# Spreading the attention's first preparation over the first FFN's last rounds, with an early flag for low parts and the weights' high parts first

## The chip, the cores and the metric

The kernel runs on one core of a Trainium2 chip. The metric is the device time of one execution in microseconds. The engines are TensorE (PE), VectorE (DVE), ScalarE (ACT), GpSimd (POOL) and SyncE (SP, which here only issues transfers). Each has a queue of its own that it works through in order; they meet through semaphores.

## The reference

A macaron block on x of 8 x 1024 rows of 128 numbers, in float32:

```
x = x + 0.5 * ffn(layernorm(x))
x = x + attn(layernorm(x))
x = x + 0.5 * ffn(layernorm(x))

ffn(x):  h = silu(x Wg^T / 127) * (x Wu^T / 127);  h Wd^T / 127     # hidden 384, int weights -127..127
attn(x): h = rmsnorm(x) * norm_w
         q, k, v = h Wq, h Wk, h Wv       # 4 query heads, 2 kv heads of 32
         q, k = l2norm(q), l2norm(k);  p = softmax(causal(q k^T * exp(log_temperature)))
         x + gate * (p v) Wo
```

## The kernel before

**Tiles.** x stays in SBUF as 64 tiles of 128 rows; a chunk `c` is four tiles, 512 rows, so there are NC = 16 chunks. Matrix products run in float16 with the inputs split into a high part and a low part (`hi`, the rounded value, and `lo`, the rest), which TensorE sums up. The integer weights are scaled by a power of two; their low part is zero unless an integer needs more bits than float16 has, and a flag, `loflag`, tells the engine's code whether to add its products. It is read into a register of TensorE, which then takes the `If` or the `Else` version of the whole FFN.

**FFN.** Each engine runs `pipeline`, a list of (offset, operation): in step i it does operation `op` for chunk i + offset. For a chunk: VectorE `stats` and `aggregate` (mean and variance), GpSimd `rstd`, ScalarE `normalise` (`XN`), TensorE `x_t` (transposes), ScalarE `x_hi`, VectorE `x_lo` (`XT`), TensorE `gate_` and `up`, ScalarE `silu` (`SG`), VectorE `hidden` (`H`), ScalarE `h_hi` (`HH`), GpSimd `h_lo` (`HL`), TensorE `down`, VectorE `residual`. TensorE's step is `gate_`(i+1), `down`(i-1), `up`(i+1), `x_t`(i+3). `H` and the other working tiles have two buffers. A step is called a round here, numbered by the chunk of its `H`. The argument `after` puts further work behind given steps.

**Attention.** A batch is two chunks ("halves"). Before its scores each half needs: statistics (`stats`, L787), reciprocal roots on GpSimd (`rstds`, L722), `normalise` (`AN`, L801, L806), `x_hi` (ACT, L646) and `x_lo` (POOL, L738) into `AS`, a transposing transfer by SP into `AXT`, the projection to q, k, v (`use`, L563, L580), `qkv_out` (ACT copies to `V` and squares to `SQ`, L652), `sums` and `norms` (DVE, L819, L827: three Newton steps for 1/norm), `unit` (`QN`, L844), `stack_hi` (ACT, L665), `stack_hi2` (DVE, L856), `stack_lo` (POOL, L743) into `ST`, and a second transposing transfer into `QKT`. `add_norm` (L810) adds the normalised input to x. The scores of a batch run in 12 groups `g`; the preparation of the next batch is laid between them, its projections in batch 0 at groups 3 and 4. For the first batch everything from the projection on happens after the FFN, in series. `by_heat` reads a second flag, `hotflag`, on each of four engines and takes the `If` or the `Else` version of the attention; with these inputs it is `Else`.

**Order in the queues.** VectorE does `stats` of the attention behind step 12 of the FFN, `normalise` and `attention_weights` behind step 15. TensorE waits for all residuals (`s_res`) before the attention. SP loads x first, then reads its flag when the attention weights are done, and then issues the transfers.

## Time and profile before

| what | value |
|---|---|
| time, median of 3 runs | 515.3 us (515.18 to 518.39) |
| profiled execution | 514.61 us, of it span 512.6 us |
| PE busy | 433.5 us (85%) |
| ACT busy | 387.7 us (76%) |
| DVE busy | 364.4 us (71%) |
| POOL busy | 244.1 us (48%) |
| chain that ended last | PE 62%, issue 11%, DVE 10%, POOL 6%, ACT 6%, DMA 3% |

Busy time is an average over the whole span; where a change acts, the windows and the timeline of that stretch count. "Issue" is time in which an engine waited for nothing that the profile shows.

### The profile page before, as it was taken

The page shows a single profiled execution, that of the slowest core. Times are in us where ns is not written, and L with a number is a line of the kernel's source. Part 1 is how long each engine was busy: PE and PEld are TensorE (multiplying, and loading weights), DVE is VectorE, ACT ScalarE, POOL GpSimd, SP SyncE. Part 2 cuts the span into 40 slices and gives each one's busy share as a digit, 9 for nine tenths or more (in the row PEclk, how much of TensorE's full clock was granted, in tenths as well). Part 3 has the DMA queues.
Part 4 walks back from the last instruction along what each step waited for, and adds up shares of the span by engine and source line. Part 5 has one row for each costly group of instructions (what it writes and reads, how often), then busy time and mean ns, then how long its engine had stood idle before and what let it go on. Part 6 is the DMA issues. An engine that isn't in the chain of part 4 may idle for free.

```text
span 512.6 us, 11225 instructions
## 1 busy us (share of the span) xinstructions
PE 433.5 (85%) x3862; PEld 234.4 (46%) x3862; DVE 364.4 (71%) x864; ACT 387.7 (76%) x552; POOL 244.1 (48%) x357
## 2 busy tenths in 40 slices
PE   0389999863088799999999999899999978999994
PEld 0237767552033253443443534434434334677674
DVE  4658887774761976886986968869755537888762
ACT  2388999631357789799788897987987977899971
POOL 4537777480264343526354454362030414777742
PEclk9999999995578999999999999999999998999998
DMA  6510000003242170711705207127060000212112
GB/s 183 168 42 3 0 0 0 1 1 47 45 81 41 32 134 2 133 35 37 130 0 108 56 0 140 25 44 122 1 120 6 2 3 1 60 44 61 52 52 61
DMA packets 85453, 26.54 MB, mean 52 GB/s; under 512 B 67872, under 2 KB 85408, under 8 KB 85408
## 3 DMA queue, kind: packets, MB, share of 16 engines
q1 hardware_dynamic: 84400, 25.76, 24.3%
q8 instruction: 26, 0.43, 0.4%
q10 hardware_dynamic: 1008, 0.20, 0.2%
q14 instruction: 19, 0.16, 0.1%
HBM read 4.98 MB, written 4.19 MB: 18 GB/s over the span
## 4 chain that ended last, share of the span: by engine, by line
PE 62%; issue 11%; DVE 10%; POOL 6%; ACT 6%; DMA 3%; POOLq 1%; SPq 0%; DVEq 0%; ACTq 0%
PE ps L384 14%; PE ps L553 11%; PE ps L534 9%; PE ps L558 9%; PE ps L424 5%; PE ps L418 5%; PE ps L377 2%; PE ps L446 2%; PE ps L580 2%; PE ps L538 2%; DVE X L815 2%; DMA AXT<-AS 1%; ACT PT L643 1%; POOL OL L227 1%; POOL HL L314 1%
## 5 line engine op out<-in xcount | busy, mean ns | idle before, releaser
L643 ACT ACTIVATE PT<-ps,k_exp 128x1024 f32<-128x1024 f32 (+1 forms) x192 | 162.7, 901 | 25.2 <-PE ps L538 19.9
L534 PE MATMUL ps<-QKT 128*128 128x512 f16 (+3 forms) x384 | 89.4, 335 | 25.0 <-DMA QKT<-ST 15.1
L384 PE MATMUL ps<-XT,WT 128*128 128x512 f16 x384 | 97.0, 391 | 8.4 <-issue 4.3
L314 POOL TENSOR_TENSOR HL<-H,HH 128x1024 f16<-128x1024 f32 x32 | 68.4, 2138 | 44.6 <-ACT HH L353 44.6
L553 PE MATMUL ps<-PT,V 128*32 128x512 f32 (+3 forms) x768 | 81.9, 498 | 0.4 <-ACT PVS L677 0.4
L558 PE MATMUL ps<-PT,ones 128*32 128x512 f32 (+3 forms) x768 | 79.6, 486 | 0.0
L263 DVE SCALAR_TENSOR_TENSOR H<-SG,k_isilu,ps 128x1536 f32<-128x1536 f32 x32 | 58.0, 1812 | 15.9 <-ACT SG L349 9.0
L534 PEld LDWEIGHTS ps<-QKT 128*128 128x128 f16 x384 | 28.4, 98 | 81.8 <-ACT PT L643 57.7
L227 POOL TENSOR_TENSOR OL<-ON,OH 128x512 f16<-128x512 f32 x16 | 19.5, 1218 | 95.9 <-ACT OH L223 95.9
L384 PEld LDWEIGHTS ps<-XT,WT 128*128 128x128 f16 x384 | 37.4, 100 | 45.4 <-issue 13.8
L217 DVE RECIPROCAL RD<-PVS 128x512 f32<-128x512 f32 x16 | 53.4, 3335 | 3.5 <-ACT PVS L677 3.5
L333 ACT ACTIVATE XN<-X,NB,RS 128x128 f32 (+1 forms) x128 | 52.4, 483 | 0.0
L349 ACT ACTIVATE SG<-ps,k_silu 128x1536 f32<-128x1536 f32 x32 | 48.8, 1526 | 3.5 <-PE ps L384 3.5
L746 POOL TENSOR_TENSOR ST<-QN,ST 128x512 f16<-128x512 f32 x16 | 20.0, 1252 | 59.6 <-ACT ST L669 59.6
L353 ACT ACTIVATE HH<-H 128x1024 f16<-128x1024 f32 x32 | 33.5, 1047 | 12.1 <-DVE H L263 12.1
L558 PEld LDWEIGHTS ps<-PT,ones 128*32 128x32 f32 x768 | 24.8, 110 | 37.5 <-issue 32.1
L268 DVE SCALAR_TENSOR_TENSOR X<-ps,k_ffn,X 128x512 f32<-128x512 f32 (+1 forms) x32 | 24.0, 750 | 23.8 <-PE ps L424 23.8
L424 PE MATMUL ps<-WD,H 128*128 128x128 f32 x256 | 37.3, 291 | 0.0
L538 PE MATMUL ps<-causal,ident 128*128 128x128 bf16 x256 | 34.9, 222 | 0.0
L821 DVE TENSOR_REDUCE SS<-SQ 128x24 f32<-128x768 f32 x16 | 15.1, 943 | 27.7 <-ACT SQ L662 27.7
L306 POOL TENSOR_TENSOR RS<-RS,nhalf 128x4 f32<-128x4 f32 x32 | 33.4, 1044 | 2.5
L580 PE MATMUL ps<-QKVO,AXT 128*128 128x256 f16 x192 | 25.5, 288 | 9.9 <-DMA AXT<-AS 9.9
(117 smaller groups left out, 696.0 us busy)
## 6 DMA issues: line engine op xcount, KB each, us to landing
X<-in_L_attn_x SPq DMA_DIRECT2D x16, 256.0 KB, 3.0
result<-X SPq DMA_DIRECT2D x16, 256.0 KB, 2.3
AXT<-AS SPq DMA_TRANSPOSE x16, 3.1
QKT<-ST SPq DMA_TRANSPOSE x16, 5.6
w_int<-in_L_ffn_w_gate SPq DMA_DIRECT2D x1, 192.0 KB, 3.7
w_int<-in_L_ffn_w_up SPq DMA_DIRECT2D x1, 192.0 KB, 4.1
w_int<-in_L_ffn_w_down SPq DMA_DIRECT2D x1, 192.0 KB, 4.6
qkvo<-in_L_attn_Wq ACTq DMA_DIRECT2D x1, 64.0 KB, 3.3
```

The source lines that it names most:

```text
L217: e.reciprocal(RD[:, :], PVS[:, 1, :]).then_inc(a_rd, 1)
L263: e.scalar_tensor_tensor(H[k % 2][:, :, :], SG[:, :, :], k_isilu[:, 0:1], U, ALU.mult, ALU.mult).then_inc(s_h, 1)
L314: e.tensor_tensor(HL[k % 2][:, :, :], H[k % 2][:, NW:, :], HH[k % 2][:, :, :], ALU.subtract).then_inc(s_hl, 1)
L333: i = e.activation(XN[k % 2][:, t, :], tile(c, t), ACT.Identity, bias=NB[k % 2][:, t:t + 1], scale=RS[k % 2][:, t:t + 1])
L349: e.activation(SG[:, :, :], G, ACT.Silu, scale=k_silu[:, 0:1]).then_inc(s_silu, 1)
L384: i = e.matmul(out[:, j, :], WT[:, wp, w * NJ + j, :], XT[k % 2][:, xp, :], start=a == 0, stop=a == len(passes) - 1)
L424: i = e.matmul(DN[:, t, :], H[k % 2][:, j, t * P:(t + 1) * P], WD[:, j, :], start=False, stop=j == NW - 1, skip_group_check=True)
L534: i_ = e.matmul(o, QKT[k % 2][:, i // TPC, NH + hp, i % TPC * P:(i % TPC + 1) * P], QKT[k % 2][:, qc, 2 * hp + h, CH - n:CH], start=True, ...
L538: i_ = e.matmul(SCORES[hp][:, h, 0:P], ident16[:, :], causal[:, :], start=False, stop=True, skip_group_check=True)
L553: e.matmul(PVD[HD * h:HD * h + HD, 0, CH - n:CH], V[k % 2][:, i, v0:v0 + HD], PT[g % 2][:, h, 0:n], start=i == 0, stop=done, skip_group_ch ...
L558: i_ = e.matmul(PVD[HD * h:HD * h + HD, 1, CH - n:CH], ones32[:, :], PT[g % 2][:, h, 0:n], start=i == 0, stop=done, skip_group_check=True)
L643: e.activation(PT[g % 2][:, 2 * hp:2 * hp + 2, 0:n], SCORES[hp][:, :, 0:n], ACT.Exp, scale=k_exp[:, 0:1]).then_inc(a_exp, 1)
```

## The change

- **Early flag.** Instead of looking at the low parts of the weights, VectorE compares the largest absolute integer with 2048, right after the column maxima. The maximum comes over TensorE in a second small transpose.
- **High part of the weights first.** VectorE makes the high part straight from the float weights, TensorE transposes it (parts 0 and 1, copied by ScalarE), and the low part follows (parts 2 and 3, copied by VectorE). `x_t`, `x_hi` and `x_lo` of chunk 0 come ahead of that. ScalarE runs one small silu early. Both flags are read into registers early.
- **Attention weights** are made ahead of step 0 of the FFN, not behind step 15.
- **Preparation of the first batch spread out.** VectorE: `stats` behind steps 7 and 8, `normalise` in four pairs of tiles behind steps 10 to 13. GpSimd: `rstds` in two parts each behind steps 8 to 11, `x_lo` behind 13 and 14. ScalarE: `x_hi` behind 12 and 14. The statistics have a buffer of their own, `abns`.
- **Joined.** SP issues both `AXT` transfers before its branch. The first projections stand in TensorE's queue behind `up` 15 and behind `down` 14 and write into PSUM banks that the FFN has left. ScalarE's `qkv_out` of half 0 comes between the last silu and the last `h_hi`. VectorE's `units` (sums, norms of one half at a time, `QN`, copies) stand behind step 15, the last `residual` and `add_norm` follow, and then the branch. TensorE waits for the last `residual` only behind the first scores.

TensorE at the start, before: the names are `ident` for the unit matrix, `w_nat` for the weights, `XN0` and `XN1` for the buffers of the normalised x.

```order
L1161 MATMUL ps<-ident32,m4 128x4
L1168 MATMUL ps<-ident16,w_nat 128x128 x18
L1171 MATMUL ps<-ident32,lomax 1x128
L377 MATMUL ps<-ident32,XN0 128x128 x4
L1176 TENSOR_LOAD loflag
L1176 ISA x2
L1179 COMPARE_AND_BRANCH
L377 MATMUL ps<-ident32,XN1 128x128 x4
```

TensorE at the start, now:

```order
L1248 MATMUL ps<-ident32,m4 128x4
L396 MATMUL ps<-ident32,XN0 128x128 x4
L1008 TENSOR_LOAD hotflag
L1008 ISA x2
L1253 TENSOR_LOAD loflag
L1253 ISA x2
L1261 MATMUL ps<-ident16,w_nat 128x128 x18
L1265 COMPARE_AND_BRANCH
L396 MATMUL ps<-ident32,XN1 128x128 x4
```

The x transpose of chunk 0 and both flag loads moved ahead of the weights' transposes; the branch stayed between them and chunk 1.

VectorE in rounds 10 to 13, now (`X` is written by `residual`):

```order
L276 SCALAR_TENSOR_TENSOR H0<-SG,k_isilu,ps 128x1536
L267 TENSOR_TENSOR XT0<-ps,XT0 128x512
L250 BN_STATS bns<-X 128x6 x4
L281 SCALAR_TENSOR_TENSOR X<-ps,k_ffn,X 128x512
L262 BN_AGGR MV1<-bns 128x2 x4
L858 TENSOR_SCALAR AN0<-X,AMV0,RMS0 128x128 x2
L276 SCALAR_TENSOR_TENSOR H1<-SG,k_isilu,ps 128x1536
L267 TENSOR_TENSOR XT1<-ps,XT1 128x512
L281 SCALAR_TENSOR_TENSOR X<-ps,k_ffn,X 128x512
L858 TENSOR_SCALAR AN0<-X,AMV0,RMS0 128x128 x2
```

The pairs of `AN` stand between a `residual` and the next `H`. Before, all eight stood behind the last `H`:

```order
L263 SCALAR_TENSOR_TENSOR H1<-SG,k_isilu,ps 128x1536
L268 SCALAR_TENSOR_TENSOR X<-ps,k_ffn,X 128x512
L806 TENSOR_SCALAR AN0<-X,AMV0,RMS0 128x128 x4
L806 TENSOR_SCALAR AN1<-X,AMV1,RMS1 128x128 x4
L1131 TENSOR_SCALAR qkvo<-qkvo,ipw 128x256
```

TensorE at the join, now, in the `Else` version (`AXT0` is half 0):

```order
L403 MATMUL ps<-XT1,WT 128x512 x6
L612 MATMUL ps<-QKVO,AXT0 128x256 x12
L445 MATMUL ps<-WT,HH0 128x128 x8
L445 MATMUL ps<-WT,HL0 128x128 x8
L451 MATMUL ps<-WD,H0 128x128 x4
L612 MATMUL ps<-QKVO,AXT1 128x256 x12
L445 MATMUL ps<-WT,HH1 128x128 x8
L445 MATMUL ps<-WT,HL1 128x128 x8
L451 MATMUL ps<-WD,H1 128x128 x4
```

The projections, which stood behind the last `down` and the branch, now stand ahead of `down` 14 and `down` 15. The diff, cut to its core:

```diff
-        w_bank = [bank[2][:, 0, :], bank[2][:, 1, :], bank[0][:, 1, :]]
+        w_bank = [bank[2][:, 0, :], bank[2][:, 1, :], bank[3][:, 1, :], bank[1][:, 1, :]]
+        w_parts = [(0, 2 * NJ), (2 * NJ, 3 * NJ), (3 * NJ, 3 * NJ + 8), (3 * NJ + 8, 6 * NJ)]
...
+            def first_out(k, c):
+
+                if ph == 0 and k == NC - 1:
+                    project_out()
...
+                if ph == 0 and k == 0:
+                    e.wait_ge(s_wt, 1)
+                    if low:
+                        e.wait_ge(s_wtl, 2)
...
+        FIRST_BANKS = [XP] + [ps[:, i, :] for i in range(3)]
...
+            if first_half is not None:
+
+                e.wait_ge(s_silu, NC)
+                for c in range(2):
+                    use(None, None, ("qkv", first_half, c))
+                return
+            first = [u for k, u in seq if k is None and u[0] != "qkv" and u[:2] != ("m", 1)]
+            late = [u for k, u in seq if k is None and u[0] != "qkv" and u not in first]
+
+            e.wait_ge(a_cp, 4)
+            e.wait_ge(s_h, NC)
+            if shift:
+                e.wait_ge(s_res, NC)
+                for u in first:
+                    use(None, None, u)
             scores(0, 0, 0, 0)
             scores(0, 0, 0, 1)
+            e.wait_ge(s_res, NC)
...
+            if first == "units":
+
+                sums(0, 0)
+                norms(0, 2, 0, 1)
+                unit(0, 10, 0, 0)
+                sums(1, 1)
+                stack_hi2(0, 0)
+                norms(10, 4, 1, 2)
+                unit(0, 20, 1, 1)
+                stack_hi2(1, 1)
+                return
...
+            hot = is_hot(e)
+            for half in range(2):
+                turn_x(e, half)
+            by_heat(e, turn, hot)
...
                             ALU.add).then_inc(s_wd, 1)
-            ffn_pool(e, 0, None, {NC - 3: lambda: att_pool(e, ("rstds", 0)),
-                               NC - 2: lambda: att_pool(e, ("rstds", 1)),
-                               NC - 1: lambda: [att_pool(e, ("x_lo", h)) for h in range(2)]})
+            ffn_pool(e, 0, None, {NC - 8: lambda: att_pool(e, ("rstds_a", 0)),
+                                  NC - 7: lambda: att_pool(e, ("rstds_b", 0)),
+                                  NC - 6: lambda: att_pool(e, ("rstds_a", 1)),
+                                  NC - 5: lambda: att_pool(e, ("rstds_b", 1)),
+                                  NC - 3: lambda: att_pool(e, ("x_lo", 0)),
+                                  NC - 2: lambda: att_pool(e, ("x_lo", 1))}, 4)
...
+            hot = is_hot(e)
+            ffn_act(e, 0, 1)
+            for r in range(2):
                 e.wait_ge(s_wpe, 3 + r)
-                lo, hi = 8 * r, min(8 * r + 8, 6 * NJ)
-                src = w_bank[r].bitcast(f16).rearrange("p (j n) -> p j n", n=P)
-                e.activation(w16[:, lo:hi, :], src[:, 0:hi - lo, :], ACT.Copy).then_inc(s_wt, 1)
+                lo, hi = w_parts[r]
+                e.activation(w16[:, lo:hi, :], w_part(r), ACT.Copy).then_inc(s_wt, 1)
             e.wait_ge(s_wready, 1)
-            ffn_act(e, 0, None, {NC - 1: lambda: [att_act(e, False, ("x_hi", h)) for h in range(2)]})
+            ffn_act(e, 0, None, {NC - 4: lambda: att_act(e, False, ("x_hi", 0)),
+                                 NC - 2: lambda: att_act(e, False, ("x_hi", 1)),
+                                 NC - 1: lambda: att_act(e, False, ("qkv_out", 1))},
+                    1, lambda: att_act(e, False, ("qkv_out", 0)))
+            for half in range(2):
+                att_act(e, False, ("stack_hi", half))
             e.wait_ge(s_wready, 2)
-            by_heat(e, att_act)
+            by_heat(e, att_act, hot)
             ffn_act(e, 1)
 
...
+            e.tensor_tensor(colmax[:, 4:5], colmax[:, 0:1], colmax[:, 1:2], ALU.max)
...
+            link(e.tensor_reduce(lo1[:, :], bank[0][0:1, 1, 0:P], AXX, ALU.max))
+            e.tensor_scalar(loflag[:, :], lo1[:, :], 2048.0, None, ALU.is_gt).then_inc(s_low, 1)
...
-            link(e.tensor_scalar(w_flt[:, 0:2 * NJ, :], w_flt[:, 0:2 * NJ, :], ipw[:, 0:1], None,
-                                 ALU.mult))
-            link(e.tensor_scalar(w_flt[:, 2 * NJ:, :], w_flt[:, 2 * NJ:, :], ipw[:, 1:2], None,
-                                 ALU.mult))
-            link(e.tensor_copy(w_nat[:, 0, :, :], w_flt[:, :, :]))
-            e.tensor_tensor(w_nat[:, 1, :, :], w_flt[:, :, :], w_nat[:, 0, :, :], ALU.subtract)\
-                .then_inc(s_wprep, 1)
+            cuts = [(0, 2 * NJ), (2 * NJ, 3 * NJ)]
+            for c, (lo, hi) in enumerate(cuts):
+                i = e.tensor_scalar(w_nat[:, 0, lo:hi, :], w_flt[:, lo:hi, :], ipw[:, c:c + 1], None, ALU.mult)
+            i.then_inc(s_wprep, 1)
+            ffn_dve(e, 0, 2)
             e.wait_ge(s_wprep, 3)
-            e.tensor_reduce(lomax[:, :], w_nat[:, 1, :, :].rearrange("p a b -> p (a b)"), AXX,
-                            ALU.max, apply_absolute_value=True).then_inc(s_wprep, 1)
-
+            for c, (lo, hi) in enumerate(cuts):
+                i = e.scalar_tensor_tensor(w_nat[:, 1, lo:hi, :], w_flt[:, lo:hi, :], ipw[:, c:c + 1],
+                                           w_nat[:, 0, lo:hi, :], ALU.mult, ALU.subtract)
+            i.then_inc(s_wprep, 1)
             link(e.tensor_scalar(k_silu[:, :], pw[:, 0:1], 1.0 / 127.0, None, ALU.mult))
             link(e.reciprocal(k_isilu[:, :], k_silu[:, :]))
             link(e.tensor_scalar(k_ffn[:, :], k_silu[:, :], k_silu[:, 0:1], 0.5 / 127.0, ALU.mult,
                                  ALU.mult))
-            link(e.tensor_scalar(k_ffn[:, :], k_ffn[:, :], pw[:, 1:2], None, ALU.mult))
-            e.wait_ge(s_wpe, 6)
-            link(e.tensor_reduce(lo1[:, :], bank[1][0:1, 1, 0:P], AXX, ALU.max))
-            e.tensor_scalar(loflag[:, :], lo1[:, :], 0.0, None, ALU.is_gt).then_inc(s_wready, 1)
+            e.tensor_scalar(k_ffn[:, :], k_ffn[:, :], pw[:, 1:2], None, ALU.mult).then_inc(s_wready, 1)
+            for r in range(2, 4):
+                e.wait_ge(s_wpe, 3 + r)
+                lo, hi = w_parts[r]
+                e.tensor_copy(w16[:, lo:hi, :], w_part(r)).then_inc(s_wtl, 1)
+            e.wait_ge(s_wready, 1)
...
+            flags = []
+            def weights_and_flag():
+                attention_weights()
+                flags.append(is_hot(e))
+            ffn_dve(e, 0, None, {-1: weights_and_flag,
+                                 NC - 9: first_rows("stats", 0),
+                                 NC - 8: first_rows("stats", 1),
+                                 NC - 6: first_rows("normalise", 0, (0, 2)),
+                                 NC - 5: first_rows("normalise", 0, (2, TPC)),
+                                 NC - 4: first_rows("normalise", 1, (0, 2)),
+                                 NC - 3: first_rows("normalise", 1, (2, TPC)),
+                                 NC - 1: lambda: att_dve(e, False, "units")}, 4)
+            for half in range(2):
+                first_rows("add_norm", half)()
+            by_heat(e, att_dve, flags[0])
             ffn_dve(e, 1)
         @block.tensor
         def _(e):
             e.wait_ge(s_const, 2)
             e.wait_ge(s_wprep, 1)
-            e.matmul(bank[0][0:4, 0, 0:P], colmax[:, :], ident32[:, :], is_transpose=True,
+            e.matmul(bank[0][0:4, 0, 0:P], colmax[:, 0:4], ident32[:, :], is_transpose=True,
+                     start=True, stop=True)
+            e.matmul(bank[0][0:1, 1, 0:P], colmax[:, 4:5], ident32[:, :], is_transpose=True,
                      start=True, stop=True).then_inc(s_wpe, 1)
             e.wait_ge(s_wprep, 2)
             e.matmul(bank[1][:, 0, 0:4], m4[:, 3:4].to_broadcast([4, P]), ident32[0:4, 0:4],
                      start=True, stop=True).then_inc(s_wpe, 1)
-            e.wait_ge(s_wprep, 3)
+            ffn_pe(e, 0, 0, 0)
+            hot = is_hot(e)
+            e.wait_ge(s_low, 1)
+            low = e.value_load(loflag[0:1, 0:1], min_val=0, max_val=1)
             blocks = [(s, j) for s in range(2) for j in range(3 * NJ)]
-            for r in range(3):
+            for r in range(4):
+                if r in (0, 2):
+                    e.wait_ge(s_wprep, 3 + r // 2)
                 dst = w_bank[r].bitcast(f16)
-                for a, (s, j) in enumerate(blocks[8 * r:8 * r + 8]):
+                for a, (s, j) in enumerate(blocks[slice(*w_parts[r])]):
                     i = e.transpose(dst[:, a * P:(a + 1) * P], w_nat[:, s, j, :], ident16[:, :])
                 i.then_inc(s_wpe, 1)
-            e.wait_ge(s_wprep, 4)
-            e.matmul(bank[1][0:1, 1, 0:P], lomax[:, :], ident32[:, :], is_transpose=True,
-                     start=True, stop=True).then_inc(s_wpe, 1)
-            ffn_pe(e, 0, 0, 0)
-            e.wait_ge(s_wt, 3)
-            e.wait_ge(s_wready, 1)
-            low = e.value_load(loflag[0:1, 0:1], min_val=0, max_val=1)
-
-            def ffn(ph):
+            def ffn(ph, after={}):
                 with e.If(low > 0):
-                    ffn_pe(e, ph, 1)
+                    ffn_pe(e, ph, 1, None, after)
                 with e.Else():
-                    ffn_pe(e, ph, 0)
-            ffn(0)
-
-            e.wait_ge(s_res, NC)
-            e.wait_ge(s_wready, 2)
-            by_heat(e, att_pe)
+                    ffn_pe(e, ph, 0, None, after)
+            def first_projection(half):
+                e.wait_ge(s_wready, 2)
+                att_pe(e, False, half)
+            ffn(0, {NC - 2: lambda: first_projection(0), NC - 1: lambda: first_projection(1)})
+            by_heat(e, att_pe, hot)
             ffn(1)
```

## Rows read from the trace of the kernel before

**Rows 1.** Windows of core 0: from:to in us, length, busy us of each engine (x instructions), PEclk, DMA share, GB/s.

```profile
60.00:100.00 40.00, 39.77 (x324) 27.79 (x321) 33.43 (x87) 34.43 (x53) 26.03 (x33) 1.00 0.00 0
130.00:140.00 10.00, 0.00 (x0) 0.00 (x0) 7.77 (x18) 2.91 (x3) 3.06 (x3) 0.50 0.19 36
219.98:253.90 33.92, 32.26 (x322) 14.41 (x320) 27.29 (x61) 29.35 (x41) 15.94 (x22) 1.00 0.37 63
```

**Rows 2.** Timeline of the start: start us, us, engine, line, operation [idle before <-releaser].

```profile
16.20 2.10 PE L1168 MATMUL ps<-ident,w_nat 128*128 128x128 f16 x18 [4.19 <-DVE w_nat L1114]
17.27 2.21 ACT L1067 ACTIVATE WT<-ps 128x1024 f16<-128x1024 f16 x3 [7.35 <-PE ps L1168]
...
24.59 1.09 PE L377 MATMUL ps<-ident,XN 128*128 128x128 f32 x4 [5.23 <-issue]
...
31.59 1.81 DVE L263 SCALAR_TENSOR_TENSOR H<-SG,k_isilu,ps 128x1536 f32<-128x1536 f32 x1 [3.37 <-PE ps L384]
```

**Rows 3.** Timeline, TensorE's jump into the second FFN.

```profile
422.71 4.44 PE L384 MATMUL ps<-XT,WT 128*128 128x512 f16 x12 [3.40 <-issue]
```

**Rows 4.** Timeline of one round in the middle of the first FFN.

```profile
85.14 1.81 DVE L263 SCALAR_TENSOR_TENSOR H<-SG,k_isilu,ps 128x1536 f32<-128x1536 f32 x1 [0.18 <-ACT SG L349]
...
88.61 0.75 DVE L268 SCALAR_TENSOR_TENSOR X<-ps,k_ffn,X 128x512 f32<-128x512 f32 x1 [1.05 <-PE ps L424]
88.62 2.14 POOL L314 TENSOR_TENSOR HL<-H,HH 128x1024 f16<-128x1024 f32 x1 [1.05 <-ACT HH L353]
...
90.01 1.81 DVE L263 SCALAR_TENSOR_TENSOR H<-SG,k_isilu,ps 128x1536 f32<-128x1536 f32 x1 [0.65 <-ACT SG L349]
```

**Rows 5.** Timeline of the first FFN's last rounds.

```profile
94.14 0.86 DVE L793 BATCH_NORM_STATS2 bns<-X 128x6 f32<-128x128 f32 x4
...
96.66 1.78 DVE L263 SCALAR_TENSOR_TENSOR H<-SG,k_isilu,ps 128x1536 f32<-128x1536 f32 x1
...
99.61 2.13 POOL L314 TENSOR_TENSOR HL<-H,HH 128x1024 f16<-128x1024 f32 x1 [3.98 <-ACT HH L353]
...
105.79 1.81 DVE L263 SCALAR_TENSOR_TENSOR H<-SG,k_isilu,ps 128x1536 f32<-128x1536 f32 x1 [0.60 <-PE ps L384]
```

**Rows 6.** One line, L806, from 108 to 116 us: duration ns min/median/max.

```profile
L806 DVE TENSOR_SCALAR AN<-X,AMV,RMS x8: 333/336/2142, 109.7 to 113.3; 128x128 f32<-128x128 f32 x8
```

**Rows 7.** Chain of waits through the join: start us, us, what.

```profile
106.95 1.07 PE ps L418 x16
108.02 0.96 PE ps L424 x8
...
109.75 4.84 DVE AN L806 x8
...
117.95 0.17 DVE k_exp L1142
...
119.48 3.87 DMA AXT<-AS
...
129.60 0.96 DVE SS L821
...
133.26 0.97 DVE QN L850
...
137.09 5.65 DMA QKT<-ST
```

**Rows 8.** Timeline of the attention's first groups.

```profile
140.10 0.86 DVE L793 BATCH_NORM_STATS2 bns<-X 128x6 f32<-128x128 f32 x4
...
142.78 1.04 PE L534 MATMUL ps<-QKT 128*128 128x512 f16 x2 [15.06 <-DMA QKT<-ST]
...
144.29 1.12 DVE L806 TENSOR_SCALAR AN<-X,AMV,RMS 128x128 f32<-128x128 f32 x4 [1.53 <-POOL RMS L734]
...
150.75 1.14 ACT L650 ACTIVATE AS<-AN 128x512 f16<-128x512 f32 x2
...
156.41 1.90 PE L580 MATMUL ps<-QKVO,AXT 128*128 128x256 f16 x12 [2.00 <-DMA AXT<-AS]
```

209 lines of the change are left out of this document (107 added, 102 removed).

## The prediction

> **What bounds the kernel now.** I read the windows first, then the timeline of the weak stretches, then the chain of waits through them. In the first FFN's middle TensorE is busy for 39.77 of 40 us, so nothing is to be had there except by doing less; between 130 and 140 us it does nothing at all, and the granted clock there is 0.50, its 1.2 GHz level [rows 1]. Two places hold the idle time. At the start, TensorE ends the transposes of the weights at 18.3, ScalarE's last copy of them ends at 19.48, and the second x transpose starts only at 24.59, with 5.23 us of idle time that no semaphore explains ("issue") [rows 2]. At the join of the first FFN and the attention, the last `H` starts at 105.79 [rows 5] and the first scores start at 142.78, after 15.06 us of waiting for the `QKT` transfer [rows 8]: 37.0 us. The chain there runs in series through `AN`, the attention weights, the `AXT` transfer, the projection, sums, norms, `QN` and the `QKT` transfer [rows 7]. Each is short; they are long only because nothing lies beside them.
>
> All sums below are made against the profiled execution: 512.6 us of span, 514.61 in all, 0.7 below the median of 515.3. Stated times of the changed kernel are on the old time axis until the sum; a gain at the start shifts them all.
>
> **1. The start: about 1.8 us less.** The gap of 19.48 to 24.59 holds the flag's load and the jump into the FFN's code. SP does its own flag load, its branch and a DMA issue from 118.12 to 119.48, so load and branch together are at most 1.4 us and the load alone about 0.8; that leaves 4.3 us for TensorE's jump [rows 2, 7]. A second jump of TensorE into such a branch left it idle for 3.40 us [rows 3]. The change loads both flags before the weights' transposes, where TensorE waited 4.19 us for VectorE anyway [rows 2], so the load costs nothing as long as that wait is there; without it, it would cost 0.8 for each flag. The jump stays, after the 18 transposes. Their low half comes later than before, since VectorE now makes it after the high half and `x_lo`; I put their end at 18.1 against 18.3, so the second x transpose starts at 18.1 + 4.3 = 22.4, 2.2 earlier. ScalarE's `XN` must be there too, after its weight copies; it is at about 19.5 and does not bind. Against this, VectorE now makes the attention weights before the first `H`: 118.12 - 114.59 = 3.5 us [rows 7], plus a flag load of 0.8, into a wait of 3.37 [rows 2]. `H` starts 0.9 late, and half of that reaches ScalarE's next silu. Net 2.2 - 0.4 = 1.8. The bounds are 0 (the fetch ends when it ended before) and 4.6 (the jump is hidden: 24.59 - 19.5, less 0.5).
>
> The Trainium skill (Advanced Engine Details and Errata, Control Flow Timing) puts a compare-and-branch at about 108 ns. No row here shows TensorE doing it so fast; by that figure the start would gain 4.6 instead of 1.8.
>
> **2. The rounds: about 4.6 us more.** A round of the FFN takes 90.01 - 85.14 = 4.87 us from `H` to `H` [rows 4]. From round 12 on that pace would put the last `H` at 90.01 + 3 x 4.87 = 104.6; it is at 105.8, so the two blocks of statistics of before, beginning at 94.14 and holding the next `H` back to 96.66, cost 1.2 net [rows 5]. The change puts much more into the rounds.
> - Statistics behind rounds 7 and 8: 2 x 1.3 us on VectorE (94.14 to the second block at 95.46, half of the stretch to 96.66) [rows 5]. VectorE waits 0.65 before an `H` [rows 4], and ScalarE takes the `H` 0.5 later than it could; the rest, 1.5, stretches the loop.
> - Pieces of `rstds` on GpSimd: some 1.7 and 1.35 us each, twice, against 1.05 us of idle time before each `HL` [rows 4]. `HL` gets late by 0.3 to 0.7 a round.
> - The normalisation in four pairs, each behind a `residual`. One such operation takes 0.34 us, or 2.14 when it is caught beside GpSimd's `HL` [rows 6], which itself takes 2.14 [rows 4]. `residual` starts at 88.61 and `HL` at 88.62 in the same round [rows 4], so VectorE comes to the pair just when `HL` has begun. The round then is `H` 1.8, to `HL` 1.15 (99.61 - 98.44) [rows 5], `HL` 2.1, and the pair 0.67: 5.7 us. Three rounds at 5.7 cost 2.5 over the pace, and the first, in which the `rstds` pieces add up, 1.7.
>
> Together 1.5 + 1.7 + 2.5 = 5.7 over the pace, less the 1.2 that before paid: the last `H` starts 4.6 later, at 110.4. The bounds are 0 and 7.
>
> **3. From the last `H` to the first scores: 37.0 becomes 17.8, so 19.2 us less.** `AXT` of half 0 has landed (half 0 is ready a round earlier; issue plus landing is 3.87 [rows 7]), so TensorE does the first projection, 1.9 us for its 12 products [rows 8], then `down` of round 14, 1.07 + 0.96 [rows 7], and VectorE the `residual`, 0.75 [rows 4], since it lies ahead of `units` in VectorE's queue: 4.7. Sum and norms as before, 133.26 - 129.60 = 3.7; half the width saves little where ten short operations follow each other. From `QN` to the `QKT` issue 137.09 - 133.26 = 3.8, and the transfer 5.65 to the scores [rows 7, 8]. 4.7 + 3.7 + 3.8 + 5.65 = 17.8. Half 1 lies beside this, as do `down` 15 and GpSimd's last `HL`. The second projection stands ahead of `down` 15 in TensorE's queue and waits for `AXT` half 1; that delays `add_norm` and no scores. The bounds are 16 (the sums do not wait for the residual) and 22 (half 1's chain or GpSimd's `HL` gets in between).
>
> **4. Behind the join: about 4.7 us given back.** Before, the statistics for the next batch began at 140.10, 2.7 us ahead of the scores, and the first half of `AN` was complete at 144.29 + 1.12 = 145.4; ScalarE took it at 150.75 [rows 8]. Now VectorE first does half 1's norms and `QN`, its copies, the last `residual` and eight operations of `add_norm` (2.3 at 0.28 each [rows 8]): by the durations of part 3 that ends 3.6 us after the first scores. Then it jumps into the attention's code. Before, that jump lay in VectorE's idle time. Priced as TensorE's 3.40 [rows 3], the statistics begin 7.0 after the scores instead of 2.7 before; `AN`'s first half, 5.3 later (145.4 - 140.1), passes ScalarE, GpSimd and SP (the 5.66 of 150.75 to 156.41 [rows 8]) and meets TensorE's projection for the next batch at 18.3 instead of 13.6. TensorE waited 2.00 there already [rows 8], so it all counts: 4.7. With a jump of 0.5 it would be 1.8; those are the bounds, with 0.5 more above for ScalarE's own jump and table load ahead of the first exponential.
>
> **Sum:** -1.8 + 4.6 - 19.2 + 4.7 = -11.7. 514.6 becomes 502.9, and 515.3 becomes **503.6 us**. The shorter gap may also save up to 1 us of products at the 1.2 GHz level; I leave it to the range.
>
> **The rivals.**
> - *The jumps are cheap.* For it: no loop of VectorE or ScalarE shows an "issue" wait of that kind. Against it: [rows 2, 3]. Start -4.6, give-back 1.8: 515.3 - 4.6 + 4.6 - 19.2 + 1.8 = 497.9. Chance 0.18.
> - *The pairs get in ahead of `HL`.* `residual` and `HL` start 0.01 us apart [rows 4]; if GpSimd is pushed later by its own new pieces, VectorE's pairs run at 0.67 and `HL` waits for no more than one of them. The rounds then cost 1.5, not 4.6: 500.5. The Trainium skill (SBUF — State Buffer, Who interferes with whom) has it that the one that issues first keeps the shared port and the other blocks; the row with 2.14 agrees for the case in which GpSimd was first, and none shows the other. Chance 0.10.
> - *The join is longer.* GpSimd's last `HL`, the late second projection or `stack_lo` get in between: 22 instead of 17.8, 507.8. Chance 0.15.
> - *The early flag brings nothing,* since the jump ends when it did: 505.4. Chance 0.05.
> - *Slower than before.* VectorE enters the attention 7 us late and stays late: the projections for the six batches after the next wait for their `AXT` too. At 4.7 each the total is 503.6 + 6 x 4.7 = 531.8; it decides from (520.5 - 503.6) / 6 = 2.8 us a batch. Against it: VectorE is busy for 27.29 of 33.92 us in a batch [rows 1], so 6.6 idle us catch up 4.7 in one batch. Chance 0.04.
>
> My forecast has 0.45; 0.03 is left for the gain being used up by something that I do not see, at 510 to 520. About 1% (5 us) is what a measurement of this kernel tells from no change. Faster by more: 0.45 + 0.18 + 0.10 + 0.15 + 0.05, less 0.02 for their upper tails, is 0.91; within 1% 0.05; slower 0.04. The range of 496 to 510 reaches from a little below the cheap jumps (both faster rivals at once would give 494.8) to the longer join with 2 us on top.
>
> **What would show it.** The second x transpose of the start at 22.4 (19.5 if jumps are cheap, 24.6 if nothing moved). `AN` operations of 2 us next to `HL`, and rounds of 5.7 us from round 10 on. 17.8 us from the last `H` to the first scores, with the sums released by the `residual`. VectorE idle with "issue" behind `add_norm`, and a wait of some 6.7 us of TensorE before the first projection of the attention's loop. Batches of 33.9 us after that. The forecast is wrong if the rounds stretch by much more than 1.5 us each, since four engines have almost no slack in them, or if the waits at batch boundaries grow.

## The result

| kernel | median of the runs | profiled execution | its span | granted clock |
|---|---|---|---|---|
| before | 515.24 us (514.79 to 518.39) | 514.61 us | 512.6 us | |
| changed | 497.03 us (495.16 to 498.07) | 498.07 us | 496.3 us | 0.972 |

The ratio is 0.9637, interval [0.9592, 0.9681]: 18.2 us less, where 11.7 was forecast. The direction and the range were right, and so was the sign of each of the four terms; the likeliest value was 6.6 us too high, and all four terms of the sum erred to the same side. The profiled execution is the slowest of the changed kernel's runs and that of before is a little below its median, so the two profiles differ by 16.3 us of span, and the terms are measured in these spans.

### The profile page after: what moved, and what is told of

Same layout as the page of the kernel before. It is cut to its first block, busy times and chain, and to the rows that moved or that the text cites. A ratio compares the mean times of both kernels' runs of the same rounds, so it can differ in the third digit from the quotient of the medians.

```text
span 496.3 us, 11174 instructions
## 1 busy us (share of the span) xinstructions
PE 433.1 (87%) x3862; PEld 232.3 (47%) x3862; DVE 369.8 (75%) x876; ACT 386.9 (78%) x552; POOL 244.0 (49%) x357
## 4 chain that ended last, share of the span: by engine, by line
PE 59%; DVE 14%; issue 11%; POOL 7%; ACT 5%; DMA 2%; POOLq 1%; DVEq 1%; SPq 0%; ACTq 0%
PE ps L403 13%; PE ps L585 11%; PE ps L590 9%; PE ps L566 9%; PE ps L451 5%; PE ps L445 5%; PE ps L474 2%; DVE X L868 2%; PE ps L396 2%; DVE H L276 2%; PE ps L570 2%; ACT SG L362 2%; PE ps L612 1%; POOL OL L240 1%; POOL RMS L786 1%
## 5 line engine op out<-in xcount | busy, mean ns | idle before, releaser
L585 PE MATMUL ps<-PT,V 128*32 128x512 f32 (+3 forms) x768 | 83.6, 507 | 1.3 <-ACT PVS L721 1.3
L858 DVE TENSOR_SCALAR AN<-X,AMV,RMS 128x128 f32<-128x128 f32 (+1 forms) x64 | 33.8, 593 | 3.5 <-POOL RMS L786 3.5
L451 PEld LDWEIGHTS ps<-WD,H 128*128 128x128 f32 x256 | 32.0, 196 | 0.0
```

Source lines behind the costliest of these rows:

```text
L451: i = e.matmul(DN[:, t, :], H[k % 2][:, j, t * P:(t + 1) * P], WD[:, j, :], start=False, stop=j == NW - 1, skip_group_check=True)
L585: e.matmul(PVD[HD * h:HD * h + HD, 0, CH - n:CH], V[k % 2][:, i, v0:v0 + HD], PT[g % 2][:, h, 0:n], start=i == 0, stop=done, skip_group_ch ...
```

## The profile after

Landmarks of each trace carry the whole comparison. H0, H1, H15: starts of the first `H`s and the last one of the first FFN; S: first scores; P: first projection for the third pair of halves ("batch 2"); F: first product of the second FFN. The columns behind H15 are stretches, in us.

| profile | second x transpose | H1 | H15 | H15 to S | S to P | P to F | F to end | span |
|---|---|---|---|---|---|---|---|---|
| before | 24.59 | 36.49 | 105.79 | 36.99 | 45.30 | 234.63 | 89.89 | 512.6 |
| changed | 21.52 | 32.87 | 105.44 | 17.12 | 48.61 | 234.39 | 90.74 | 496.3 |
| start alone | 21.36 | 34.50 | 103.79 | 37.48 | 44.72 | 234.65 | 90.56 | 511.2 |
| flag late | 24.11 | 35.46 | 107.91 | 17.09 | 47.68 | 234.09 | 89.73 | 496.5 |
| pairs ahead of `HL` | 20.19 | 31.54 | 100.86 | 17.11 | 48.20 | 234.23 | 89.80 | 490.2 |
| low swapped | 19.66 | 31.17 | 103.64 | 19.01 | 46.98 | 231.07 | 92.90 | 493.6 |
| hot swapped | 21.57 | 32.93 | 105.41 | 17.08 | 47.54 | 239.71 | 90.76 | 500.5 |
| exp early | 21.07 | 32.42 | 104.99 | 17.13 | 50.62 | 234.65 | 89.91 | 497.3 |
| stats early | 21.44 | 32.77 | 105.25 | 17.09 | 48.30 | 234.55 | 89.81 | 495.0 |
| these five together | 19.72 | 31.25 | 100.58 | 17.07 | 47.71 | 234.33 | 90.71 | 490.4 |
| changed, again | 21.36 | 32.70 | 105.17 | 17.10 | 49.36 | 234.11 | 87.86 | 493.6 |
| adds early | 20.94 | 32.28 | 104.86 | 17.09 | 49.62 | 234.07 | 90.76 | 496.4 |
| exp and adds early | 21.08 | 32.42 | 104.89 | 17.11 | 49.16 | 234.10 | 90.84 | 496.1 |
| best | 19.22 | 30.73 | 100.06 | 19.27 | 46.56 | 231.06 | 92.05 | 489.0 |

The changed kernel stands there twice: between its two profiles S to P differs by 0.75 and F to end by 2.9. Smaller differences in those columns tell nothing. The four terms, changed against before: start -3.6 (H1), rounds +3.3 (H1 to H15), join -19.9, behind the join +3.9 (S to the end). The last one is the least certain: against the second profile of the changed kernel it would be +1.5, and up to P alone it is +3.3 in the one and +4.1 in the other.

**The start**, timeline: start, duration, engine, line, operation, idle time before and what ended it.

```profile
16.91 1.14 PE L1261 MATMUL ps<-ident,w_nat 128*128 128x128 f16 x9 [0.91 <-DVE w_nat L1189]
...
21.52 1.09 PE L396 MATMUL ps<-ident,XN 128*128 128x128 f32 x4 [3.47 <-issue]
...
28.50 1.81 DVE L276 SCALAR_TENSOR_TENSOR H<-SG,k_isilu,ps 128x1536 f32<-128x1536 f32 x1 [0.86 <-issue]
```

The transposes end at 18.05 (forecast 18.1), then come 3.47 us of idle time without the flag's load; [rows 2] had 5.23 with it. The jump itself is not the same in every program with this start: 3.40 in e9, 2.75 in e10 and 2.42 in e3.

**The rounds**, the four pairs of `AN` on VectorE and `HL` on GpSimd.

```profile
81.17 2.13 POOL L327 TENSOR_TENSOR HL<-H,HH 128x1024 f16<-128x1024 f32 x1
81.91 1.73 DVE L858 TENSOR_SCALAR AN<-X,AMV,RMS 128x128 f32<-128x128 f32 x2
...
86.54 2.52 DVE L858 TENSOR_SCALAR AN<-X,AMV,RMS 128x128 f32<-128x128 f32 x2
86.59 2.13 POOL L327 TENSOR_TENSOR HL<-H,HH 128x1024 f16<-128x1024 f32 x1
...
91.95 2.13 POOL L327 TENSOR_TENSOR HL<-H,HH 128x1024 f16<-128x1024 f32 x1 [1.95 <-ACT HH L366]
92.02 2.40 DVE L858 TENSOR_SCALAR AN<-X,AMV,RMS 128x128 f32<-128x128 f32 x2
...
97.97 2.67 DVE L858 TENSOR_SCALAR AN<-X,AMV,RMS 128x128 f32<-128x128 f32 x2
```

Each pair meets `HL` and takes 1.73 to 2.67 us instead of 2 x 0.34 [rows 6]; the fourth meets `x_lo` of GpSimd as well (from 99.41, 1.16 us). This is what the forecast said from one row with 2.14. The rounds from H10 on take 6.15, 5.42, 5.37, 6.22 and 4.87 us; the three from H7 to H10, which hold the statistics, take 15.35 together, where before took 14.52.

**The middle of the FFN and the join**, windows (from:to, length, busy us of PE, PEld, DVE, ACT, POOL, PEclk, DMA share, GB/s).

```profile
60.00:100.00 40.00, 37.82 (x298) 25.66 (x297) 37.84 (x86) 32.76 (x48) 30.63 (x43) 1.00 0.00 1
110.00:120.00 10.00, 3.46 (x36) 2.88 (x36) 9.20 (x28) 2.88 (x4) 3.51 (x3) 0.86 0.13 30
```

Against [rows 1], VectorE went from 33.43 to 37.84 busy us of 40, TensorE from 39.77 to 37.82: the two are as busy as each other over this window, part of VectorE's time being the wait beside `HL`. From the first pair (81.91) to H14 (100.57) VectorE waits once, 0.56 us, so there it has become the bound. At the join VectorE is now busy for 9.20 of 10 us, so that stretch is VectorE's too. Its chain of waits (start, us, what):

```profile
105.50 1.47 PE ps L612 x12
...
108.85 0.75 DVE X L281
109.60 0.87 DVE SS L874
...
113.86 0.96 DVE QN L900
```

`H` to sums 4.2 (forecast 4.7), sums to `QN` 4.3 (3.7; one operation of it, L877 on 24 columns, took 1.17 us, and 0.24 for the other half: it ran beside GpSimd's last `HL`, from 109.51 to 111.64, and ended with it), from there to the issue of the `QKT` transfer at 117.83 4.0 (3.8), and 4.7 to the scores at 122.56 (5.65): 17.1 against 17.8. As forecast, the residual of round 14 stands ahead of the sums.

**Behind the join**, timeline of ScalarE, VectorE and TensorE.

```profile
123.84 1.28 ACT L687 ACT_TABLE_LOAD   x1 [2.20 <-issue]
125.13 2.12 ACT L687 ACTIVATE PT<-ps,k_exp 128x1024 f32<-128x1024 f32 x2
...
135.53 0.63 ACT L694 ACTIVATE AS<-AN 128x512 f16<-128x512 f32 x1 [1.87 <-DVE AN L858]
```

```profile
122.98 0.74 DVE L281 SCALAR_TENSOR_TENSOR X<-ps,k_ffn,X 128x512 f32<-128x512 f32 x1
123.64 2.12 DVE L868 TENSOR_SCALAR X<-X,A,B 128x128 f32<-128x128 f32 x8
126.12 0.87 DVE L845 BATCH_NORM_STATS2 abns<-X 128x6 f32<-128x128 f32 x4 [0.35 <-issue]
...
133.43 2.06 DVE L858 TENSOR_SCALAR AN<-X,AMV,RMS 128x128 f32<-128x128 f32 x4 [1.99 <-POOL RMS L786]
```

```profile
126.39 0.80 PE L566 MATMUL ps<-QKT 128*128 128x384 f16 x2 [1.53 <-ACT PT L687]
128.27 1.94 PE L585 MATMUL ps<-PT,V 128*32 128x512 f32 x8
129.98 1.42 PE L590 MATMUL ps<-PT,ones 128*32 128x512 f32 x8
...
138.41 1.47 PE L612 MATMUL ps<-QKVO,AXT 128*128 128x256 f16 x12 [0.22 <-DMA AXT<-AS]
```

Three engines are late here at once. ScalarE jumps and loads its table, so the first exponential comes 2.57 us after the scores (before: 1.29). VectorE's statistics come 3.56 after them (before: 2.68 ahead). And TensorE's products with `V` and with the ones take 1.94 and 1.42 us for eight where the same ones took 1.06 and 1.04 before, since they now fall into the stretch with a granted clock of 0.50, its 1.2 GHz level (0.50 from 127.5 to 130.5, 0.87 in the next microsecond). Windows from the scores on, of the changed kernel:

```profile
122.56:127.56 5.00, 3.46 (x13) 1.47 (x14) 4.51 (x20) 3.52 (x4) 1.12 (x3) 0.50 0.70 152
127.56:132.56 5.00, 5.00 (x36) 1.78 (x38) 2.32 (x13) 2.36 (x4) 4.53 (x12) 0.68 0.05 12
```

and of the kernel before:

```profile
142.78:147.78 5.00, 4.82 (x24) 2.10 (x28) 1.50 (x6) 3.56 (x4) 4.60 (x11) 0.57 0.68 128
147.78:152.78 5.00, 5.00 (x64) 2.03 (x53) 4.83 (x24) 3.46 (x7) 1.32 (x2) 1.00 0.01 2
```

TensorE was busy for 4.82 of the first five us before and is for 3.46 now, with the pause of 1.53 ahead of the x384 scores in it; the full level of the clock comes later. The projection for batch 1 comes at 15.85 after the scores (16.57 in the second profile of the changed kernel); 13.63 before, 18.3 in the forecast.

What releases its `AXT` transfer (issued at 134.93) is GpSimd's `x_lo`, 133.74 to 134.90. Two chains reach that operation within 0.05 us of each other (0.3 in e9): ScalarE's `AS`, which stands behind a late exponential and ends at 133.66, and GpSimd's own queue, in which both halves' `rstds` stand ahead of it, from 127.48 to 133.71. Taking one of the two away leaves the other.

## The experiments

Each was timed beside the kernel before on the same chip (medians there 515.96 for e1 to e4, 517.26 for e5 to e8, 514.55 for e9 to e11, 514.66 for e12). The chips differ by more than some effects, so what is compared with the changed kernel is the ratio to before, 0.9637 [0.9592, 0.9681] there, and the stretches of the profiles. Of the variants of the changed kernel only e8 and e11 are clear of it by the ratio alone.

**e1_start_only.** The kernel before with the start of the changed one and nothing else: high part first, early flag, chunk 0 ahead of the weights, attention weights still behind step 15.

```diff
+        w_parts = [(0, 2 * NJ), (2 * NJ, 3 * NJ), (3 * NJ, 3 * NJ + 8), (3 * NJ + 8, 6 * NJ)]
+            e.tensor_scalar(loflag[:, :], lo1[:, :], 2048.0, None, ALU.is_gt).then_inc(s_low, 1)
+            ffn_pe(e, 0, 0, 0)
+            e.wait_ge(s_low, 1)
+            low = e.value_load(loflag[0:1, 0:1], min_val=0, max_val=1)
```

> The kernel before with the new start alone (early low-part flag, high parts of the weights first, chunk 0 transposed early); the attention's preparation stays behind the FFN. Theory A: the start and the rest of the change add up. In the changed kernel the FFN's second H is 3.6 us earlier than before (32.87 against 36.49), and here the attention weights do not stand before the first H, so I expect a gain of 3.5 to 4.5 us, about 511 us. Theory B: the start's gain is used up by a wait later in the FFN and only counts together with the joined preparation: under 1 us of gain.

513.11 us (511.23 to 513.87), ratio 0.9944 [0.9917, 0.9972]: 2.9 us less, and in the profile 2.0 by H1 and by H15. That is less than the changed kernel's 3.6 by H1, and the difference has a place:

```profile
21.36 1.09 PE L386 MATMUL ps<-ident,XN 128*128 128x128 f32 x4 [3.30 <-issue]
22.23 1.06 PE L393 MATMUL ps<-XT,WT 128*128 128x512 f16 x2
24.79 4.45 PE L393 MATMUL ps<-XT,WT 128*128 128x512 f16 x10 [1.50 <-issue]
```

A second pause of 1.50 us lies behind the first two gate products; the changed kernel has none. Why, no run here tells. All of the start's gain arrives at H15, so the rounds hand it on in full.

**e2_flag_late.** The changed kernel with the low flag loaded where it was.

```diff
-            e.wait_ge(s_low, 1)
-            low = e.value_load(loflag[0:1, 0:1], min_val=0, max_val=1)
...
+            e.wait_ge(s_wt, 2)
+            e.wait_ge(s_wtl, 2)
+            e.wait_ge(s_wready, 1)
+            low = e.value_load(loflag[0:1, 0:1], min_val=0, max_val=1)
```

> The changed kernel, but TensorE reads the low-part flag behind the weights' transposes and copies, where the kernel before read it. Theory A: the flag's position is worth its load (about 0.8 us) and the wait for the copies (0.9 us), since the jump stays where it is: second x transpose at 23.0 to 23.5 instead of 21.5, total 1.5 to 2 us longer. Theory B: the load's latency is the whole gap of the kernel before, and the jump costs nothing: second x transpose at 24.5, 3 us longer.

499.02 us (497.84 to 499.73), 0.969 [0.9628, 0.9752]. The second x transpose starts at 24.11, near the 24.5 of theory B, behind 6.13 us of "issue". That does not make the jump free: 3.47 of it stand there without the load too. The load, with the waits that the edit puts ahead of it, accounts for the other 2.7, where theory A had 1.7. The early load is worth 2.6 us there, in H1, and 2.5 in H15; in the medians 2.0.

**e3_pairs_first.** The pairs of `AN` stand behind `x_lo` and ahead of the `residual` in the same rounds, so that `HL` has not begun.

```diff
+            def pair(k, c):
+                if ph == 0 and 10 <= k <= 13:
+                    h, part = divmod(k - 10, 2)
+                    att_dve(e, False, ("normalise", h, (2 * part, 2 * part + 2)))
...
-            pipeline(e, [(0, hidden), (2, x_lo), (1, last_o_norm), (5, stats), (5, sums_there),
+            pipeline(e, [(0, hidden), (2, x_lo), (0, pair), (1, last_o_norm), (5, stats), (5, sums_there),
```

> The changed kernel with each pair of AN operations one place earlier in VectorE's queue: behind x_lo and ahead of the residual, in the same rounds 10 to 13. Same work. Theory A (the pair is caught beside GpSimd's HL, 1.7 to 2.7 us instead of 0.67): the pairs take 0.6 to 0.7 us each, rounds 11 to 14 shrink from 5.4-6.2 to about 4.9-5.1, and the last H is 3 to 4 us earlier; total about 493.5. Theory B (the rounds are long because of the added work, wherever it stands): the last H moves by less than 1 us.

493.68 us (492.01 to 494.49), 0.959 [0.9531, 0.9649].

```profile
78.41 0.59 DVE L863 TENSOR_SCALAR AN<-X,AMV,RMS 128x128 f32<-128x128 f32 x2
79.82 0.75 DVE L281 SCALAR_TENSOR_TENSOR X<-ps,k_ffn,X 128x512 f32<-128x512 f32 x1
79.85 2.13 POOL L332 TENSOR_TENSOR HL<-H,HH 128x1024 f16<-128x1024 f32 x1
...
88.46 0.61 DVE L863 TENSOR_SCALAR AN<-X,AMV,RMS 128x128 f32<-128x128 f32 x2 [0.25 <-POOL RMS L791]
```

The same instructions take 0.59 to 0.61 us a pair instead of 1.73 to 2.67, and H1 to H15 takes 69.32, as in the kernel before (69.30), where it took 72.57. H10 to H15 is where it is gained: 24.78 instead of 28.03. So the whole +3.3 of the rounds is taken back by moving the pairs away from `HL`. Statistics and `rstds` are not free for that: H7 to H10 takes 15.35, 0.8 more than before, as in the changed kernel, and H10 to H15 still some 0.5 more than before without its own statistics (25.51 less their 1.2). They cost together what before paid for its statistics. By the medians e3 is 3.4 below the changed kernel, by the ratios 2.4, and its profile also has a start that is 1.3 earlier, which the edit does not touch.

**e4_low_swapped.** TensorE's two versions of the FFN change places, so that the one in use is the `If`.

```diff
-                with e.If(low > 0):
-                    ffn_pe(e, ph, 1, None, after)
+                with e.If(low < 1):
+                    ffn_pe(e, ph, 0, None, after)
```

> The changed kernel with the two versions of the FFN swapped in TensorE's code: the version that runs (no low part) comes straight behind the branch, the other behind it. Theory A: the 3.47 us before the second x transpose and the 1.73 us before the second FFN's first product are TensorE's jump to code that is far away; straight on, the transpose comes at 19.3 (released by XN) and the second FFN starts 1.5 us earlier. Total 3 to 4 us less. Theory B: the wait is that of a branch itself or of the new code in any case, near or far: no change.

495.42 us (493.64 to 495.52), 0.9608 [0.9547, 0.9669].

```profile
19.66 1.11 PE L396 MATMUL ps<-ident,XN 128*128 128x128 f32 x4 [1.30 <-ACT XN L346]
```

No "issue" is left ahead of the second x transpose: a semaphore of ScalarE releases it now. The pause ahead of the second FFN is gone as well (P to F 231.07 instead of 234.39). So the pause belongs to the jump over the unused version. The trace's DMA records say what lies in it: in the changed kernel's pauses a packet of 16 KB of the queue named "instruction" is fetched (18.84 to 19.96 at the start, 402.91 to 404.01 ahead of the second FFN), and in e4 none is in either place. The other programs agree: one in each such pause, none where the near version follows (the starts of e8 and e11).

The total fell by 1.6 us by the medians and 1.5 by the ratios, not by the 3 to 4 expected. Ahead of the second FFN little of the gain is kept: the first `H` there now stands directly behind VectorE's other work.

```profile
407.08 0.38 DVE L262 BATCH_NORM_AGGREGATE MV<-bns 128x2 f32<-128x6 f32 x4
407.38 1.78 DVE L276 SCALAR_TENSOR_TENSOR H<-SG,k_isilu,ps 128x1536 f32<-128x1536 f32 x1
```

P to this `H` is 237.75, against 239.73 and 238.44 in the two profiles of the changed kernel. And something took part of the start's gain back: the `QKT` transfers, issued at the same distance from H15, landed after 6.1 to 6.5 us instead of 4.6 to 5.5, and the scores came 1.9 later. Two "instruction" packets run at once over the issue of the first of these transfers in e4 and e11 (the later one ends 1.1 us behind it); in the changed kernel and in e8 the last one has ended before. That they are the cause was not tested.

**e5_hot_swapped.** The same for the attention's two versions, on all four engines that have them.

```diff
-            with e.If(hot > 0):
-                att(e, True)
+            with e.If(hot < 1):
+                att(e, False)
```

> The changed kernel with the two versions of the attention swapped in the code of TensorE, VectorE, ScalarE and SP: the one that runs comes straight behind the branch. Theory A: the 2.20 us (issue) of ScalarE between stack_hi and the table load ahead of the first exponential is its far jump, and now lies on the path; it vanishes, the first exponential starts 1.3 us earlier (1.2 instead of 2.6 after the first scores begin), and total time falls by 1 to 2 us. Theory B: ScalarE waits there for something else, or the later AXT wait makes up for it: under 0.5 us.

502.17 us (499.93 to 503.12), 0.9712 [0.9648, 0.9776]: 5.1 us more than the changed kernel by the medians, 3.9 by the ratios. The first exponential came at 1.27 as hoped, but the jump only moved to where the attention is left:

```profile
409.74 5.28 PE L403 MATMUL ps<-XT,WT 128*128 128x512 f16 x12 [8.46 <-issue]
415.11 1.81 DVE L276 SCALAR_TENSOR_TENSOR H<-SG,k_isilu,ps 128x1536 f32<-128x1536 f32 x1 [5.44 <-issue]
```

TensorE stands still for 8.46 us there, instead of 3.16 in the changed kernel. It makes two far jumps in a row, out of the attention and into the `Else` version of the second FFN, and three "instruction" packets of 16 KB begin in the pause (401.64, 405.23, 405.60). The exit alone is no dearer than the other jumps, as e8 shows, where the FFN's near version follows:

```profile
399.69 4.37 PE L408 MATMUL ps<-XT,WT 128*128 128x512 f16 x12 [3.09 <-issue]
```

Two jumps cost 8.46, more than 3.09 and 3.16 together; why was not tested. VectorE's 5.44 is no jump: its `H` needs the products that TensorE begins at 409.74 and ends at 415.02. The pause lies between two stretches that have TensorE full.

**e6_exp_early.** ScalarE does one exponential of a single column between its two `stack_hi`, so that the table is loaded before the jump.

```diff
+            e.activation(warm[:, :], lt_t[:, :], ACT.Exp)
```

> The changed kernel with one tiny exponential on ScalarE between the two stack_hi, where it is idle, so that the table load of 1.28 us happens there and not ahead of the first scores' exponential. If that load is on the path behind the join, the first exponential starts 1.2 us earlier relative to the scores and the total falls by about 1.2 us; if the batch's AXT sets the time instead (the projection for batch 1 came 15.85 us after the scores, 2.2 later than before), it changes nothing.

496.14 us (492.93 to 499.07), 0.9584 [0.9519, 0.965]. The exponential came at 1.27, yet P came at 50.62: no gain in this profile, which is the slowest of the four runs; the ratio leaves room for a small one. `AS` of the first half is made 1.5 us earlier against the scores, but GpSimd's `x_lo` for it is not:

```profile
131.14 0.63 ACT L694 ACTIVATE AS<-AN 128x512 f16<-128x512 f32 x1
...
133.18 0.20 POOL L788 TENSOR_TENSOR B<-rv,AMV 128x4 f32<-128x4 f32 x1
133.33 1.15 POOL L792 TENSOR_TENSOR AS<-AN,AS 128x512 f16<-128x512 f32 x1
```

It stands behind the `rstds` of both halves in GpSimd's queue, and the `AXT` transfer goes out at 134.50, 12.38 after the scores. So here the late statistics carry the term, through GpSimd.

**e7_stats_early.** Statistics for batch 1 directly behind `units`, ahead of the jump.

```diff
                 stack_hi2(1, 1)
+                stats(2, 2, 0)
+                stats(3, 3, 1)
                 return
```

> The changed kernel with the statistics for batch 1 ahead of the last residual and add_norm in VectorE's queue, directly behind units. My prediction put the give-back behind the join at 4.7 us, through the late statistics. If that path (statistics, reciprocal roots, AN, AS, AXT, projection) carries the 3.3 us that are lost by batch 1, then bringing the statistics forward by 3 us brings the projection to 13.6 instead of 15.85 us after the scores and the total down by 2 us. If the late exponentials and the low granted clock carry it, the total falls by under 0.5 us.

496.29 us (491.98 to 497.7), 0.9586 [0.951, 0.9662]. The statistics came 3.1 us earlier, the `AXT` transfer for batch 1 at the same 12.39 after the scores: the second `AN` started at 133.31, as in the changed kernel (133.43), again behind GpSimd. GpSimd's `rstds` start as late as before, now released by `add_norm`, which still reads `A` and `B` that `rstds` writes:

```profile
127.27 0.28 POOL L777 TENSOR_TENSOR rv<-AMV,eps_ln 128x4 f32<-128x4 f32 x1 [3.85 <-DVE X L868]
```

The edit has a side effect too: the last `residual` comes behind the statistics, and TensorE waits 1.53 us for it behind the first scores.

**e8_all.** e3 to e7 in one kernel.

> The changed kernel with all of it: pairs ahead of the residual, both versions swapped, the early exponential, the early statistics. If the pieces lie one after the other on the path: 3.3 (pairs) + 2.7 (swapped FFN) + 2 to 3 (behind the join) = 8 to 9 us below the changed kernel, about 488.5. If the ones behind the join overlap: about 490.5.

492.43 us (491.33 to 493.15), 0.9532 [0.9473, 0.9591]. That is 1.9 above the more cautious of the two expectations. It has e3's rounds; the swapped attention takes back what the swapped FFN gives (P to F 234.33).

**e9_after_again.** The changed kernel beside the next two.

> The changed kernel itself, on the chip of the next two, as their yardstick. Both theories: 496 to 498 us, first attention scores some 122.5 us into the span, the transfer that transposes for batch 1 issued 12.4 us after them, the projection of batch 2 at +48.6.

496.15 us (495.44 to 496.97), 0.966 [0.9591, 0.9729].

**e10_add_early.** e7, and `add_norm` of both halves behind the last two `H`, ahead of the residual and of the jump.

```diff
+            def add_first(k, c):
+                if ph == 0 and k >= NC - 2:
+                    h = k - (NC - 2)
+                    att_dve(e, False, ("add_norm", h))
```

> VectorE does both additions of the norm (add_norm) of the first two batches in its queue behind the last two H, ahead of its far jump, and statistics for the third and fourth batch directly behind the last round. Theory A (what is given back behind the join comes by the chain add_norm, then GpSimd's rstds, then ScalarE's AN, then the transfer that transposes): that transfer for batch 1 is issued at about +10 us behind the first scores instead of +12.4, the first projections at about +13.6, batch 2's at +46 to +47, and the kernel takes about 2 us less than the changed kernel, near 495. Rival B (TensorE's granted clock in that stretch, or the order on ScalarE, sets it): the statistics come early, the projections stay where they are, and the time is within 0.5 us of the changed kernel. Rival C: the additions wait for their inputs and hold up the residual of the last rounds, and the first scores come more than 1 us later.

497.67 us (496.64 to 498.44), 0.9679 [0.9607, 0.975], 1.5 us above e9 on the same chip and inside the noise: no gain. GpSimd is free early here (its last `rstds` operation ends at 130.0), and `AN` did come early, complete at 131.2, so the wait of `rstds` for `add_norm` is real. It alone does not set the transfer, since `AS` was not made:

```profile
125.00 0.72 DVE L281 SCALAR_TENSOR_TENSOR X<-ps,k_ffn,X 128x512 f32<-128x512 f32 x1
129.09 2.14 DVE L863 TENSOR_SCALAR AN<-X,AMV,RMS 128x128 f32<-128x128 f32 x8 [3.37 <-issue]
```

```profile
125.78 0.82 PE L571 MATMUL ps<-QKT 128*128 128x384 f16 x2 [1.54 <-DVE X L281]
...
127.60 1.94 PE L590 MATMUL ps<-PT,V 128*32 128x512 f32 x8
129.30 1.94 PE L595 MATMUL ps<-PT,ones 128*32 128x512 f32 x8
```

```profile
131.97 1.26 ACT L692 ACTIVATE PT<-ps,k_exp 128x512 f32<-128x512 f32 x2 [3.37 <-PE ps L575]
133.13 1.14 ACT L699 ACTIVATE AS<-AN 128x512 f16<-128x512 f32 x2
```

`AS` stands in ScalarE's queue behind an exponential, which waits for scores, which wait behind products at the 1.2 GHz level, which waited for the last `residual`, now behind the statistics. And with `add_norm` gone from behind the residual, VectorE's jump lies open: 3.37 us.

**e11_best.** e3, e4, e6 and e10.

> The pieces that helped by themselves, together: pairs of AN ahead of HL, TensorE's FFN branch swapped so that the near side is the first FFN, ScalarE's Exp ahead of its jump, and the additions of the last experiment. If they add (3.3 us of pairs, some 1.6 to 2.7 of the swap, 2 of the additions): 488 to 490 us. If the waits behind the join take each other's place: 491 to 493, where the version with all four earlier pieces stood (492.43).

488.56 us (487.46 to 490.76), 0.9496 [0.9428, 0.9565], the fastest of all, and within what was expected if the pieces add. They don't add as expected, though. Against its neighbour e9: H15 5.1 earlier (2.0 of it at the start, 3.1 in the rounds), H15 to P 0.6 less, P to F 3.0 less, F to end 4.2 more. What the profiles show of its gain is the rounds and the first jump of the FFN; for the second jump and for what was done behind the join they show nothing that can be told from noise. (S to P fell by 2.8, H15 to S rose by 2.2, as in e4.) The profiled execution is the slowest of its five.

**e12_exp_add.** e6 and e10 together.

> Early statistics and additions on VectorE together with the early Exp on ScalarE, nothing else. Each by itself left the transfer that transposes for batch 1 at 12.4 to 13.1 us behind the first scores. Theory D (several engines are late at once and each covers the other: ScalarE's Exp holds up TensorE's later scores, and by them AS in ScalarE's own queue; VectorE's AN is late as well): with both gone the transfer is issued at +10 to +11, batch 1's first projection comes at +13.6 to +14.5, batch 2's at +46.5 to +47.5, and the kernel takes about 494 to 495 us against 496.2 to 497.0 of the changed kernel. Rival E (what the best version gained there came from its pairs or its swapped branch, not from these two): the transfer stays at +12.4 or later and the time stays at 496 to 497.

497.3 us (495.71 to 499.07), 0.9661 [0.9604, 0.9718]: the theory that these two only cover each other falls too.

```profile
123.27 2.18 ACT L692 ACTIVATE PT<-ps,k_exp 128x1024 f32<-128x1024 f32 x2 [2.17 <-PE ps L575]
126.88 1.75 ACT L692 ACTIVATE PT<-ps,k_exp 128x768 f32<-128x768 f32 x2 [1.43 <-PE ps L575]
```

The first pair of exponentials is early, the next waits for TensorE, which again waits 1.51 us for the residual and then runs its products in 1.94 and 1.93. With each cover lifted another one shows: first exponential, residual, clock level, `AN`. What stays open is how much they hold together: the version with the residual ahead of the statistics, and both ahead of `AN`, was not run, nor was one with GpSimd's `x_lo` of the first half ahead of the second half's `rstds`, and the level of the clock in that stretch was not separated from the rest.

## Why the prediction was right, and where it was off

1. **Start: -1.8 forecast, -3.6 measured.** The step was right up to the end of the transposes (18.05). Three sizes were off. The jump took 3.47 and not the 4.3 that I had taken as the rest of the pause in [rows 2] after a load of 0.8; 3.40 stood in [rows 3] and would have been the better price: 0.8. The load was taken too short by as much: 5.23 - 3.47 leaves 1.8 for it in [rows 2], not 0.8. The 0.4 for VectorE's attention weights ahead of the first `H` did not arise, H0 being earlier by as much as the x transpose, 3.1. And 0.5 came between H0 and H1. e4 shows that the pause is the jump. The Trainium skill's 108 ns for a compare-and-branch (Advanced Engine Details and Errata, Control Flow Timing) is met by none of these jumps over whole versions of the FFN; where no "issue" pause shows, in e4, the code followed the branch directly.
2. **Rounds: +4.6 forecast, +3.3 measured.** Mechanism right, and shown by e3: pairs of 1.7 to 2.7 us beside `HL`, 0.6 away from it. Too high was the 1.5 for statistics: H7 to H10 grew by 0.8. The pairs and `rstds` were priced at 1.7 + 2.5 = 4.2, and H10 to H15 grew by 3.7 over before without its own statistics (28.03 - 25.51 + 1.2). The rival that the pairs get ahead of `HL` did not occur by itself but was the experiment: it was priced at 500.5, 3.1 below the forecast, and e3 gained 3.4 over the changed kernel by its median. By the Trainium skill (SBUF — State Buffer, Who interferes with whom) the one that issues first keeps the shared port and the other blocks. Three pairs, begun 0.07 to 0.74 us behind `HL`, agree. The one begun 0.05 us ahead of it (86.54) does not, by the starts that the profile records: its first operation took 2.27 us, and `HL` its usual 2.13. Only pairs wholly ahead of `HL` took 0.59 to 0.61.
3. **Join: -19.2 forecast, -19.9 measured.** Right in every step; the transfer took 4.7 instead of 5.65, the norms 0.6 more. The rival of a join of 22 did not come, though GpSimd's last `HL` did get in between: beside it one small operation took 0.9 longer (1.17 against 0.24). That 17.1 is so near 17.8 is in part errors that cancel.
4. **Behind the join: +4.7 forecast, +3.9 measured.** The size is near, by luck in part: the second profile of the changed kernel has +1.5, and the forecast's own terms give 4.3 and not 4.7 (7.0 + 5.3 + 5.66 = 18.0, where it has 18.3). The chain described, statistics, `rstds`, `AN`, `AS`, transfer, is there, with other times: the statistics came 3.56 after the scores and not 7.0, `AN`'s first half was complete 5.3 later as forecast (131.44), and from there it was 7.0 to the projection and not 5.66. VectorE's jump does cost what was assumed, 3.37 to 3.79 us (e10 to e12), but it runs while the eight operations of `add_norm` (2.12 us) still execute, and only 0.35 was open. What was missing in the forecast is ScalarE's side (first exponential 1.3 later, of which 0.5 had been named), the products at 1.2 GHz, and that GpSimd does the `rstds` of both halves, 6.2 us, before the first `x_lo`. The chain through the first two and the one through the third end within 0.05 us of each other. e6 lifts the first exponential alone and leaves GpSimd, e10 frees GpSimd and leaves the rest; neither gains, and e12, with both edits, doesn't either. So none of the named causes carries the term by itself.
5. **It is not paid in every batch.** The projection is 2.2 later than before in batch 1 and 3.3 in batch 2, and no later after that: P to F takes 234.39 against 234.63. So the rival at 531.8 is excluded, as argued from VectorE's idle time.
6. The rival of cheap jumps named 497.9, almost the measured time, but for a wrong reason: jumps were not cheap (3.47, and 3.16 ahead of the second FFN). That a number fits does not confirm its story; the landmarks do.

Of the 6.6 us between forecast and median, 4.6 are these terms (1.8, 1.3, 0.7, 0.8), 1.7 is that the profiled execution lies 1.0 above the median of its kernel and that of before 0.6 below its own, and 0.3 is rounding and time outside the span.

## What to carry to other kernels

Work laid into another engine's full loop is best placed by what runs beside it: the same four pairs of instructions cost 3.3 us more beside GpSimd's long operation than a little earlier. Put the version of the code that is used next to the branch where an engine is waited for, and look where the jump goes instead. When a stretch has several engines late at once, taking one away shows the next: look in the queue of every engine for what stands ahead of the operation that releases the transfer, GpSimd's too.

## What the runs showed of the hardware that was not expected

- The pause of a jump over an unused version: 2.4 to 3.5 us on TensorE for the FFN's, 3.09 for leaving the attention past its long `Else` (e8), 8.46 for that and the FFN's in a row (e5), 1.9 to 2.6 on ScalarE, 3.4 to 3.8 on VectorE; none seen if the code follows the branch (e4). A packet of 16 KB of the "instruction" queue lies in TensorE's pauses.
- VectorE's jump overlaps with instructions that it has already been given: 0.35 us open behind `add_norm` (1.01 in e4), 3.37 without it.
- A pause of 1.50 us behind the first two gate products in one program (e1), and none in another with the same instructions there.
- First `QKT` transfers that landed 1.9 and 2.1 us later in the two programs with the FFN swapped in TensorE's code and the attention not (e4, e11); e8, with the attention swapped too, did not show it for the first of them.
